# Low parts of the transposed weights by a TensorE product and a ScalarE copy, in a fused attention and FP4 feed-forward kernel

## The reference

```python
V = X @ W_V
scores = jnp.einsum('bqd,bkd->bqk', _xpos(X @ W_Q), _xpos(X @ W_K, downscale=True))
p_attn = jax.nn.softmax(scores, axis=-1) * D[None, :, :]
x = _layernorm(x + jnp.einsum('bqk,bkv->bqv', p_attn, V))
# fp4_linear: quantise and dequantise both operands per block of 16
h = silu(fp4_linear(x, w_gate)) * fp4_linear(x, w_up)      # 704 wide
x = _layernorm(x + fp4_linear(h, w_down))
```

## Time and profile before

| | |
|---|---|
| median of the runs | 996.42 us |
| lowest and highest | 993.7, 997.01 us |
| the profiled execution's own time | 996.81 us |
| its span, first to last instruction | 995.0 us |
| mean granted TensorE clock | 0.998 of full speed |
| busy: TensorE (PE) | 967.9 us, 97% |
| busy: VectorE (DVE) | 866.8 us, 87% |
| busy: GpSimd (POOL) | 829.2 us, 83% |
| busy: ScalarE (ACT) | 638.8 us, 64% |

### The profile page before, as it was taken

One profiled execution on the slowest core, in us unless ns is written; L12 is line 12 of the kernel. 1 busy time (PEld: TensorE's weight loads), 2 busy tenths in 40 slices (PEclk: granted clock), 3 DMA queues, 4 the chain that ended last, 5 costly groups with the idle time before them and its releaser, 6 DMA issues.

```text
span 995.0 us, 20531 instructions
## 1 busy us (share of the span) xinstructions
PE 967.9 (97%) x6002; PEld 871.3 (88%) x6002; DVE 866.8 (87%) x2003; ACT 638.8 (64%) x1575; POOL 829.2 (83%) x1034
## 2 busy tenths in 40 slices
PE   8899999999999999999999999999999999999996
PEld 7788898989888898998989899898988989889885
DVE  7978988988888888998888898898898898899985
ACT  3656676676657667666666666666665766777753
POOL 5988889798888989799798888979888798887753
PEclk9999999999999999999999999999999999999999
DMA  8123244342532433333342424423243242233300
GB/s 314 43 86 128 81 142 129 102 133 75 156 116 83 145 103 121 128 105 110 116 154 79 133 88 121 150 91 128 85 152 115 91 144 79 88 106 107 107 17 22
DMA packets 116112, 111.27 MB, mean 112 GB/s; under 512 B 12576, under 2 KB 93728, under 8 KB 114080
## 3 DMA queue, kind: packets, MB, share of 16 engines
q1 hardware_dynamic: 115312, 108.91, 34.1%
q10 hardware_dynamic: 688, 1.05, 0.3%
HBM read 69.53 MB, written 40.37 MB: 110 GB/s over the span
## 4 chain that ended last, share of the span: by engine, by line
POOL 30%; PE 29%; DVE 17%; issue 16%; ACT 4%; DMA 2%; SPq 0%; POOLq 0%; ACTq 0%; DVEq 0%
POOL prob L2315 5%; POOL h L2200 5%; PE ps_g L608 4%; PE ps_g L609 4%; PE ps_g L610 4%; POOL xv L2200 3%; POOL xt_l L2229 3%; PE ps_oy L608 3%; DVE rot_a L1607 3%; PE ps_oy L610 3%; PE ps_oy L609 3%; POOL rot_a L2213 3%; POOL pt_l L2287 2%; POOL rs L2274 2%; DVE turned L1702 2%
## 5 line engine op out<-in xcount | busy, mean ns | idle before, releaser
L2200 POOL TENSOR_TENSOR h<-h,hsc 128x704 f32<-128x704 f32 x126 | 168.6, 1338 | 45.5 <-DVE h L1676 26.5
L2315 POOL TENSOR_TENSOR prob<-prob,decay_t 128x512 f32<-128x512 f32 x128 | 164.8, 1300 | 1.9 <-ACT prob L1200 1.9
L608 PE MATMUL ps_oy<-v_h,pt_h 128*128 128x256 f32 x512 | 149.7, 292 | 2.0 <-POOL pt_l L2287 1.5
L608 PE MATMUL ps_g<-wgu_h,xqt_h 128*128 128x480 f32 (+1 forms) x380 | 148.7, 391 | 2.0 <-DVE xqt_l L1731 0.9
L609 PE MATMUL ps_oy<-v_l,pt_h 128*128 128x256 f32 x512 | 144.7, 283 | 0.0
L610 PE MATMUL ps_oy<-v_h,pt_l 128*128 128x256 f32 x512 | 144.5, 282 | 0.0
L610 PE MATMUL ps_g<-wgu_h,xqt_l 128*128 128x480 f32 (+1 forms) x380 | 142.5, 375 | 0.0
L609 PE MATMUL ps_g<-wgu_l,xqt_h 128*128 128x480 f32 (+1 forms) x380 | 142.3, 374 | 0.0
L608 PEld LDWEIGHTS ps_oy<-v_h,pt_h 128*128 128x128 f32 x512 | 97.6, 191 | 6.4 <-DVE pt_l L1712 3.1
L608 PE MATMUL ps_s<-k_h,q_h 128*128 128x512 f32 x256 | 102.9, 402 | 0.0
L1683 DVE TENSOR_TENSOR ht_l<-ps_t,ht_h 128x512 fp32r<-128x512 f32 x126 | 58.3, 486 | 50.8 <-ACT ht_h L1258 50.7
(11 more groups left out here) (277 smaller groups left out, 3102.3 us busy)
## 6 DMA issues: line engine op xcount, KB each, us to landing
parking<-turned SPq DMA_DIRECT2D x122, 256.0 KB, 2.1
landing<-parking SPq DMA_DIRECT2D x488, 64.0 KB, 2.0
rope_t<-rope SPq DMA_DIRECT2D x15, 1024.0 KB, 5.2
xres<-x SPq DMA_DIRECT2D x64, 128.0 KB, 2.1
out<-yout SPq DMA_DIRECT2D x63, 128.0 KB, 2.0
xin<-x_t SPq DMA_DIRECT2D x14, 512.0 KB, 4.0
first_rope<-rope SPq DMA_DIRECT2D x2, 512.0 KB, 8.2
decay_t<-decay SPq DMA_DIRECT2D x1, 960.0 KB, 12.1
```

The source lines that it names most:

```text
L608: pe.matmul(dst, a_h, b_h, start=(start and i == 0), stop=False)
L2200: return tt(blocks(dst), blocks(src), sc[:, which, at:at + n].unsqueeze(2).to_broadcast([P, n, QB]), ALU.mult)
L2315: tt(prob[:, keys], prob[:, keys], decay_t[:, lo:lo + CW], ALU.mult).then_inc(decayed, 1)
```

## The change

The nine `weight_low(g)` move from VectorE to a product on TensorE and a copy on ScalarE. After `weight_high(g)`, the new `weight_rest(g)` multiplies the high part by minus the identity and adds it onto the bank, which then holds the low part; the new ScalarE `weight_low(g)` copies it out. `wtl_done` keeps its meaning. The transposes are written as matmuls with `is_transpose`, with start at the first and stop at the last of the four. The two semaphores for the rest of the first values become one that counts to two, which makes room for `wrest_done`. `w_turned` and `w_turned_bank` only name the views that `weight_high` used.

```diff
+        def w_turned(t, g):
+            if g < FC:
+                r = LAST if g == FC - 1 else P
+                return t[:, :, :, g * P:g * P + r].rearrange("p a g n -> p g a n")
+            m = g - FC
+            return t[:, 2 * m:2 * m + 2, :].rearrange("p c (a n) -> p c a n", a=2)
...
@@ TensorE
-                transposes(w_bank(g), sources, wt_done)
+                for n, src in enumerate(sources):
+                    r = src.shape[0]
+                    mm = pe.matmul(w_bank(g)[:, n, 0:r], src, ident[0:r, 0:r], start=n == 0, stop=n == 3, is_transpose=True)
+                mm.then_inc(wt_done, 1)
+            def weight_rest(g):
+                pe.wait_ge(wth_done, g + 1)
+                pe.matmul(w_turned_bank(g), minus_ident, w_turned(wgu_h if g < FC else wd_h, g), start=False, stop=True,
+                          skip_group_check=True).then_inc(wrest_done, 1)
...
             scores(0, 0)
+            weight_rest(0)
+            weight_rest(1)
             pe.wait_ge(first_rot_done[2], 2)
...
             prob_transposes(0, 1)
+            weight_rest(2)
+            weight_rest(3)
             values_product_first(0)
             weight_transposes(4)
             values_product_second(0)
             weight_transposes(5)
+            weight_rest(4)
+            weight_rest(5)
             weight_transposes(6)
             scores(2, 0)
+            weight_rest(6)
             weight_transposes(7)
+            weight_rest(7)
             prob_transposes(1, 0)
             weight_transposes(8)
+            weight_rest(8)
             scores(2, 1)
@@ ScalarE
+            def weight_low(g):
+                act.wait_ge(wrest_done, g + 1)
+                nc.scalar.copy(w_turned(wgu_l if g < FC else wd_l, g), w_turned_bank(g)).then_inc(wtl_done, 1)
...
             weight_high(0)
             weight_high(1)
+            weight_low(0)
+            weight_low(1)
             first_rotated_high(2, 1)
...
             exponential(1)
             weight_high(3)
+            weight_low(2)
+            weight_low(3)
             weight_high(4)
             weight_high(5)
+            weight_low(4)
+            weight_low(5)
             r1_mean(0)
             r1_squares(0)
             weight_high(6)
+            weight_low(6)
             weight_high(7)
+            weight_low(7)
             weight_high(8)
+            weight_low(8)
             rotated_high(0, 1)
@@ VectorE
-            def weight_low(g):
...
-                tt(dst, src, hi.bitcast(F32), ALU.subtract).then_inc(wtl_done, 1)
...
             weight_grid(1)
-            weight_low(0)
             weight_reciprocals(3)
             weight_reciprocals(4)
             weight_shift(2)
-            weight_low(1)
             weight_grid(2)
             row_max(0)
...
             row_max(1)
-            weight_low(2)
             probs_low(0, 1)
-            weight_low(3)
-            weight_low(4)
             first_residual(0)
-            weight_low(5)
-            weight_low(6)
-            weight_low(7)
-            weight_low(8)
             row_max(2)
```

More of the change, by code:

```diff
@@ L236, in build @@
         minus_ident_set = sem("minus_ident_set")
-        first_vrest_done = [sem("first_vrest_done%d" % c) for c in range(2)]
+        first_vrest_done = sem("first_vrest_done")
         first_vl_done = [sem("first_vl_done%d" % c) for c in range(2)]
@@ L266, in build @@
         wth_done = sem("wth_done")
+        wrest_done = sem("wrest_done")
         max_done = sem("max_done")
@@ L460, in w_bank, with w_turned_bank @@
             return ps_g[:, g % 2].rearrange("p (a n) -> p a n", a=4)
+        def w_turned(t, g):
[4 more added lines that the diff above has]
+            return t[:, 2 * m:2 * m + 2, :].rearrange("p c (a n) -> p c a n", a=2)
+        def w_turned_bank(g):
+            if g < FC:
+                r = LAST if g == FC - 1 else P
+                return w_bank(g).rearrange("p (g a) n -> p g a n", g=2)[:, :, :, 0:r]
+            return w_bank(g).rearrange("p (c a) n -> p c a n", c=2)
         @block.sync
@@ L651, in first_values_rest @@
                                    skip_group_check=True)
-                mm.then_inc(first_vrest_done[c], 1)
+                mm.then_inc(first_vrest_done, 1)
             def unread_products(dst, n):
@@ L1061, in first_values_low @@
             def first_values_low(c):
-                act.wait_ge(first_vrest_done[c], 1)
+                act.wait_ge(first_vrest_done, c + 1)
                 at = half_of(0) * (NT * D) + c * 4 * D
@@ L1080, in weight_high @@
                 act.wait_ge(wt_done, g + 1)
[L1081 to L1089, removed]
+                nc.scalar.copy(w_turned(wgu_h if g < FC else wd_h, g), w_turned_bank(g)).then_inc(wth_done, 1)
+            def weight_low(g):
+                act.wait_ge(wrest_done, g + 1)
+                nc.scalar.copy(w_turned(wgu_l if g < FC else wd_l, g), w_turned_bank(g)).then_inc(wtl_done, 1)
             def new_x_high(c):
```

## The result

The changed kernel takes 1001.6 us (median of 6 runs, 1000.44 to 1002.52), the kernel before 996.57 us (6 runs). The ratio is 1.0049, 95% interval 1.0038 to 1.0060: slower by 4.9 us, 3.8 to 6.0. Timed again later (e11) it is 1.0047 (1.0035 to 1.0059). The forecast was 1002.4 us and slower.

The account below looks back on a forecast made before the run. The prediction took TensorE's exit from the prologue, at project_next(1, 2), to set the end. The first stall's +2.91 us and the later ping-pong brought its shift to +5.96, hence 1002.4 us against the median; 8 in 10 range 999.3 to 1005.0.

Parts of the forecast that it names:

- What bounds it: Prologue before 54.2 us: what counts is when TensorE leaves it; from project_next(1, 2) at 54.27 it works back to back.
- That a shift stays: After project_next(1, 2): a shift there shifts the end, save up to 0.6 us; wrong if that stretch shortens over 1 us.
- Groups 0 and 1: Early prologue: products free on TensorE; VectorE's relief (0.4) and GpSimd's delay (0.1 to 0.2) nearly cancel; weight_high(3) stays at 46.62.
- The first stall: Groups 2 and 3: weight_rest(3) waits for weight_high(3), so values_product_first(0) starts at 47.66 instead of 44.75, +2.91 us.
- Groups 4 to 8: Behind the first values: TensorE and ScalarE alternate (ping-pong) through products and copies, putting project_next(1, 2) at 60.23, +5.96 us.
- The old path: Residual, statistics, new_x_low(2) after tile 0's last values product: ready at about 57.3, under the 60.2 of TensorE's own queue.
- The sum: Whole kernel: +5.96 us on the profiled 996.81 gives 1002.8, or 1002.4 against the median; +4.9 to +6.8 with unknowns.
- Relief of VectorE as the governing effect: Rival, VectorE between 32.7 and 43.66: two pieces of 0.60 leave the chain, 1.2 us off, 995.2; 7%.
- Only the first stall counts: Rival: products 6 to 8 find ScalarE ahead, new_x_low(2) path is last at 57.3, +3.0 us, 999.4; 12%.
- The clock: Rival, new stretch from 45 to 60: granted clock falls, at most 1.7 us lost, +7.7, 1004.1; 8%.

Follow-up runs that it names:

- e11: The changed kernel itself, unaltered, timed and profiled again against the kernel before: 1000.84 us, ratio 1.0047.
- e10: Kernel before with only group 1's low part by product, its ScalarE copy behind weight_magnitude(2); group 0 stays on VectorE: 995.12 us, ratio 0.9989.
- e12: The kernel of e10 run once more, against the kernel before: ratio 0.9993.
- e1: Changed kernel with only groups 0 and 1 by product and ScalarE copy, groups 2 to 8 back on VectorE: 997.03 us, ratio 1.000 against before.
- e7: As e1, but the low copies of groups 0 and 1 stand behind first_rotated_high(2, 1), not ahead: 996.67 us, ratio 0.9990 against before.
- e5: Changed kernel with the products of groups 2 and 3 moved behind values_product_first(0): 999.78 us, ratio 1.0027 against before.
- e6: Changed kernel with only groups 6 to 8 by product and ScalarE copy, groups 0 to 5 on VectorE: 999.13 us, ratio 1.0016 against before.
- e2: Changed kernel with groups 0 to 5 by product and ScalarE copy, groups 6 to 8 on VectorE: 999.75 us, ratio 1.003 against before.
- e4: Kernel before plus unread products and copies standing in for groups 2 to 8, without their waits; VectorE still makes all low parts: 999.49 us, ratio 1.0023.
- e3: Changed kernel with groups 0 and 1 back on VectorE, groups 2 to 8 by product and ScalarE copy: 1002.55 us, ratio 1.0056 against before.

## Why the prediction was right, step by step

*What bounds it.* Right. The projection moved from 54.27 to 59.82 and the stretch behind it stayed full.

*That a shift stays.* The prediction named a sign against it: the stretch from the projection to the end over 1 us shorter than before. It is 940.73 us before, 938.78 in the changed kernel and 938.57 in e11, so by that sign the claim fails. But the sign was ill chosen: the same stretch is 939.82 in e10 and 942.69 in e12, one kernel. As far as executions of one kernel agree, up to exponential(7), the shift stays (5.58 us).

*Groups 0 and 1.* Right for TensorE (the products ran at 30.08 and cost nothing) and for GpSimd (32.17, forecast 32.23). I took VectorE's relief and GpSimd's delay as cancelling and left weight_high(3) at 46.62; it was at 46.25. That step of the sum was wrong: the relief came through nearly in full (0.37 of 0.4; 0.31 by the common start), and GpSimd's delay does not reach weight_high(3) but new_x_low(2), where e1 shows it. That 0.37 is nearly all of what the forecast of project_next(1, 2), 60.23, is too late (0.41). What I did not see is which of the two would govern without the larger loss: e1 shows that it is GpSimd's queue, and e7 that moving two copies frees it.

*The first stall.* Right: 47.22 for 47.66, with 1.95 us of idle TensorE. e5 confirms that order, not work, makes it.

*Groups 4 to 8.* Right in kind and size. From values_product_first(0) to the projection I had 12.57 us and the trace has 12.60. The products are 0.40 long, 0.50 behind a wait (0.39 and 0.47 taken), the low copies 0.59.

*The old path.* Right: xt_l is ready at 56.9 (57.3 forecast) and releases nothing. In that sum the end of the values, 51.38, is 3.07 behind 48.31 where the shift was 2.91; nothing hung on it.

*The sum.* +5.55 between the profiles' projections (5.96 forecast), +4.9 us in the runs (3.8 to 6.0). The 5.6 lie inside that interval; up to exponential(7) nothing of them is recovered, and whether 0.7 us is recovered behind it can't be told, as executions differ there by more.

*The rivals.* Relief of VectorE as the governing effect is refuted, but its mechanism exists and is worth 0.5 us once nothing stands in its way. "Only the first stall counts" is refuted by e6. The clock: the price was right (at most 1.7 forecast, 1.5 in e2), but neither profile of the changed kernel has the fall. The argument against it, that the prologue's holes of 1.5 us bring none, does not reach holes of two: e2 fell behind one. The Trainium skill (TensorE: Matmul & The Clock Gate, "What's actually happening") has the clock fall after an idle window whose phase is not tied to the kernel. That e2 fell and three others, with the same hole, did not, agrees with the free phase; whether such a hole is what the page calls an idle window no run here shows.

## What to carry to other kernels

Moving the work of one busy engine onto two others adds hand-overs, and each is a wait in a queue that runs in order: ask what stands behind the waiting instruction, not only what the instruction costs. Here seven products and copies (groups 2 to 8) held up the prologue by 1.0 us as bare work, by the trace of e4, and by 5.9 with their waits. The one group of nine that was worth moving had both: the engine that gives the work away is on the chain there, and those that take it have a gap at that very place.

## What the runs showed of the hardware

TensorE's granted clock fell to 0.50 for 3.4 us (47.8 to 51.2) in one execution (e2), 0.9 us after a hole of 1.96 us had ended, and did not in the profiles of the changed kernel, e11 and e3 with the same hole. The 0.50 is the level of 1.2 GHz. A product added onto a bank that transposes have just filled costs what a product of 512 columns costs elsewhere in this prologue: 0.40 us long, 0.24 to the next matmul (54.12 to 54.36), against 0.40 and 0.23 (58.08 in the changed kernel).
